# Down products of an eight-expert feed-forward layer with the weights stationary, turned back in the next block

## What is computed

```
h = jax.nn.silu(xf @ gw.T) * (xf @ uw.T)
eo = h @ dw.T
out = out + mask[:, None].astype(xf.dtype) * eo * mean_w
```

## Time and profile before

| | before |
|---|---|
| median of 3 runs | 470.59 us |
| the profiled execution's own time | 470.76 us |
| its span in the trace | 468.9 us |
| PE busy | 445.0 us, 95% of the span |
| DVE busy | 301.5 us |
| ACT busy | 278.3 us |
| GpSimd busy | 140.9 us |
| mean granted PE clock | 0.989 |

### The profile page before, as it was taken

The page is one execution under the profiler, slowest core; times in us unless marked ns, Lnnn a source line. Parts: engine busy times, 40 slices in busy tenths (PEclk is TensorE's granted clock), DMA queues, the critical chain, the costliest instruction groups (busy, mean ns, idle before and its releaser), DMA issues.

```text
span 468.9 us, 9096 instructions
## 1 busy us (share of the span) xinstructions
PE 445.0 (95%) x2825; PEld 366.2 (78%) x2825; DVE 301.5 (64%) x743; ACT 278.3 (59%) x886; POOL 140.9 (30%) x172
## 2 busy tenths in 40 slices
PE   7899999999999999899999999999999999999980
PEld 4566565666666665589999999999999999999980
DVE  3776879898988977877647466376464663763320
ACT  2488878878787788355456455454554554554230
POOL 5301116262727243663050130410501304105022
PEclk9999999999999999999999999999999999999995
DMA  5740182040303042436845565557455654113002
GB/s 160 227 108 5 49 313 73 5 112 8 109 11 107 11 123 65 121 105 181 277 85 155 166 129 143 141 151 213 78 148 167 130 148 95 17 40 41 1 8 31
DMA packets 24668, 49.92 MB, mean 106 GB/s; under 512 B 5730, under 2 KB 15494, under 8 KB 24474
## 3 DMA queue, kind: packets, MB, share of 16 engines
q1 hardware_dynamic: 12858, 22.95, 16.3%
q10 hardware_dynamic: 5616, 19.40, 13.9%
q0 software_dynamic: 6144, 6.97, 9.4%
HBM read 39.16 MB, written 13.20 MB: 112 GB/s over the span
## 4 chain that ended last, share of the span: by engine, by line
PE 73%; DVE 7%; DMA 6%; ACT 5%; issue 3%; POOL 2%; SPq 1%; ACTq 0%; POOLq 0%; DVEq 0%
PE b_small L779 9%; PE b_o L779 9%; PE b_s L764 7%; PE b_s L765 7%; PE b_s L768 7%; PE b_s L487 6%; PE b_pv L510 4%; ACT probs L912 3%; PE b_proj L566 3%; PE b_pt L496 3%; PE b_s L485 3%; PE b_pt L765 2%; PE b_pt L764 2%; PE b_pt L768 2%; PE b_proj L540 2%
## 5 line engine op out<-in xcount | busy, mean ns | idle before, releaser
L912 ACT ACTIVATE probs<-b_s,negmax 100x100 f32<-100x100 f32 x256 | 85.7, 361 | 19.3 <-DVE negmax L1230 19.1
L1452 POOL DMA_INDIRECT out<-y_sb,idnow x32 | 47.8, 1494 | 163.6 <-ACT y_sb L958 158.8
L945 ACT CAST h_hi<-h_sb 128x448 fp32r<-128x448 f32 x64 | 36.3, 567 | 87.1 <-DVE h_sb L1314 87.1
L764 PE MATMUL b_s<-x_hi,w_lo 128*128 128x448 f32 x192 | 70.6, 368 | 0.0
L765 PE MATMUL b_s<-x_hi,w_hi 128*128 128x448 f32 x192 | 69.7, 363 | 0.0
L768 PE MATMUL b_s<-x_lo,w_hi 128*128 128x448 f32 x192 | 69.2, 360 | 0.0
L1207 DVE TENSOR_TENSOR w_lo<-w_raw,w_hi 128x1024 fp32r<-128x1024 f32 x48 | 58.8, 1224 | 13.7 <-ACT w_hi L876 13.7
L1318 DVE TENSOR_TENSOR h_lo<-h_sb,h_hi 128x448 fp32r<-128x448 f32 x64 | 40.1, 626 | 40.5 <-ACT h_hi L945 40.5
L912 ACT ACTIVATION_READ_ACCUMULATOR probs<-b_s,negmax 100x1 f32 x256 | 56.9, 222 | 0.0
L487 PE MATMUL b_s<-kblk,qrot 128*100 128x400 f32 x128 | 53.6, 499 | 0.0
L876 ACT CAST w_hi<-w_raw 128x1024 fp32r<-128x1024 f32 x48 | 50.4, 1049 | 0.0
(11 more groups left out here) (180 smaller groups left out, 978.2 us busy)
## 6 DMA issues: line engine op xcount, KB each, us to landing
w_raw<-in_ffw ACTq DMA_DIRECT2D x36, 512.0 KB, 3.9
w_raw<-in_ffw SPq DMA_DIRECT2D x12, 512.0 KB, 5.5
slots<-in_padrows SPq DMA_DIRECT2D x9, 449.8 KB, 4.7
xin<-slots SPq DMA_DIRECT2D x9, 449.8 KB, 4.4
kblk<-krot SPq DMA_DIRECT2D x120, 12.5 KB, 1.8
out<-x_all SPq DMA_DIRECT2D x8, 200.0 KB
ctx_all<-in_ctxT SPq DMA_DIRECT2D x1, 1200.0 KB, 6.8
x_all<-in_x SPq DMA_DIRECT2D x1, 1200.0 KB
```

The source lines that it names most:

```text
L764: pe.matmul(o, wl[:, c, cols], x_hi[:, c, :], start=(c == 0), stop=False)
L912: m = nc.scalar.activation(probs[:, N % 3, h, :], b_s[N % 3][0:S, h * S:(h + 1) * S], ACT.Exp, bias=negmax[:, N % 4, h:h + 1], accum_out=p ...
L945: nc.scalar.copy(h_hi[:, f, :], h_sb[:, f % 2, :]).then_inc(s_hhi, 1)
L1452: G.indirect_dma_start(out, bass.IndirectOffsetOnAxis(idnow[:, n:n + 1], 0), y_sb[:, n, :], None, bounds_check=TOK + TILE - 1, oob_is_err= ...
```

## The change

The down product changes sides. The down weights are now stationary (128x128) and the 448 rows of `h` move, so that one chunk takes 6 matmuls (2 output column blocks c, 3 part products) and the result has output columns on the partitions: column block 0 in `b_o`, block 1 in `b_small`. ACT scales it into the new buffer `yT` (`take_columns`, 2 copies of 128x448). In the next block, behind `hidden` of f = 0, PE turns it back with 8 transposes (`output_transpose`) into `b_xt`, and ACT copies it behind its f = 0 work into `y_sb` (`take_rows`, 2 copies of 112x512). The last expert keeps the old `project_down` and `take_output`; its block still runs `output_transpose` and `take_rows` for the tile before it. The first block transposes a `yT` that nobody reads.

```diff
+            def columns_down(par, t, f, chunks=range(DC)):
+                pe.wait_ge(s_hlo, FC * t + f + 1)
+                if f == 0:
+                    pe.wait_ge(s_y, GRP * t + GRP)
+                wh, wl = wpart(w_hi[par])[2], wpart(w_lo[par])[2]
+                for c in chunks:
+                    for k, (left, right) in enumerate(((wh, h_hi), (wl, h_hi), (wh, h_lo))):
+                        m = pe.matmul(b_y[c][:, 0:TILE], left[:, f, c * P:(c + 1) * P], right[:, f, :],
+                                      start=(f == 0 and k == 0), stop=(f == FC - 1 and k == 2))
+                    if f == FC - 1:
+                        m.then_inc(s_down, 1)
+
+            def output_transpose(t):
+                pe.wait_ge(s_yT, DC * t + DC)
+                for g in range(GRP):
+                    for c in range(DC):
+                        m = pe.transpose(b_xt[g // 2][0:ROWS, g % 2 * D + c * P:g % 2 * D + (c + 1) * P],
+                                         yT[:, c, g * ROWS:(g + 1) * ROWS], ident[:, :])
+                    if g % 2:
+                        m.then_inc(s_yt, 1)
+
...
                     hidden(par, t, f)
+                    if f == 0:
+                        output_transpose(lo if last else t)
                     if f >= 3:
-                        project_down(par, t, f - 3)
+                        (project_down if last else columns_down)(par, t, f - 3)
+                if not last:
+                    for c in range(DC):
+                        for f in range(FC - 3, FC):
+                            columns_down(par, t, f, (c,))
+                    return
...
+            def take_columns(t, e):
+                a.wait_ge(s_mean, 1)
+                for c in range(DC):
+                    a.wait_ge(s_down, DC * t + c + 1)
+                    nc.scalar.activation(yT[:, c, :], b_y[c][:, 0:TILE], ACT.Copy, scale=meanw[:, e:e + 1]
+                                         ).then_inc(s_yT, 1)
+
+            def take_rows(t):
+                a.wait_ge(s_idnow, t)
+                for n in range(GRP // 2):
+                    a.wait_ge(s_yt, 2 * t + n + 1)
+                    nc.scalar.copy(y_sb[:, 2 * n:2 * n + 2, :].rearrange("p g d -> p (g d)"), b_xt[n][0:ROWS, :]
+                                   ).then_inc(s_y, 2)
...
                 for f in range(FC):
                     silu(t, f)
                     hidden_high(t, f)
+                    if f == 0 and follow:
+                        take_rows(t)
                     if split and f < WCH:
                         weights_high(e, par, f)
...
                 if e < E - 1:
-                    take_output(t, e)
+                    take_columns(t, e)
...
+            V.memset(yT[:, :, :].rearrange("p c t -> p (c t)"), 0.0).then_inc(s_yT, DC)
```

More of the change, by code:

```diff
@@ L223, in build @@
         y_sb = sb("y_sb", [ROWS, GRP, D])
+        yT = sb("yT", [P, DC, TILE])
         b_small = bank("b_small")
@@ L343, in build @@
         s_y = sem("s_y")
+        s_yT = sem("s_yT")
+        s_yt = sem("s_yt")
         s_add = sem("s_add")
@@ L783, in project_down, with block @@
                         m.then_inc(s_down, 1)
-            def block(t, par, last):
+            def columns_down(par, t, f, chunks=range(DC)):
[17 more added lines that the diff above has]
+                        m.then_inc(s_yt, 1)
+            def block(t, par, last, lo):
                 for f in range(FC):
@@ L800, in block @@
                 project_down(par, t, FC - 1, range(2, GRP))
-                if last:
-                    tile_transpose(t + 1)
+                tile_transpose(t + 1)
             warm(2)
@@ L809, in _ @@
                 with pe.Fori(lo, hi) as t:
-                    block(t, e % 2, e == E - 1)
+                    block(t, e % 2, e == E - 1, lo)
         @block.scalar
@@ L959, in take_output, with step @@
                                          ACT.Copy, scale=meanw[0:ROWS, e:e + 1]).then_inc(s_y, 1)
-            def step(t, e, par, split, again):
+            def take_columns(t, e):
[10 more added lines that the diff above has]
+                                   ).then_inc(s_y, 2)
+            def step(t, e, par, split, again, follow):
                 for f in range(FC):
@@ L974, in step @@
                 if e < E - 1:
-                    take_output(t, e)
+                    take_columns(t, e)
             def expert(e, par, again):
                 lo, hi, end = tiles_of(a, e)
-                step(lo, e, par, True, again)
+                step(lo, e, par, True, again, e > 0)
                 with a.If(end - lo), a.Fori(lo + 1, hi) as t:
-                    step(t, e, par, False, False)
+                    step(t, e, par, False, False, True)
             def last_expert(e, par):
-                lo, hi, _ = tiles_of(a, e)
-                with a.Fori(lo, hi) as t:
-                    step(t, e, par, False, False)
+                lo, hi, end = tiles_of(a, e)
+                step(lo, e, par, False, False, True)
+                with a.If(end - lo), a.Fori(lo + 1, hi) as t:
+                    step(t, e, par, False, False, False)
             x_high(0)
```

## The result

The changed kernel takes 467.24 us (median of 6 runs, 466.06 to 468.65), the kernel before 470.77 (6 runs, 470.26 to 472.55). The ratio is 0.9917 with a 95% interval of 0.9902 to 0.9931, so it is about 3.9 us faster (3.3 to 4.6); the two medians differ by 3.5. The forecast was 4.1 us less, 466.5, range 465.2 to 469.0.

A forecast was written before the change was run, and what follows sets the result against it. PE's instruction count and spacing were taken to bound the feed-forward blocks. Down products -11.48 us and new transposes +7.36 us gave -4.1 us, so 466.5 us was forecast, range 465.2 to 469.0.

The forecast's parts named there:

- Down products: On PE in seven blocks, 48 at 0.2002 us replace 96 short ones: 1.64 us less per block, 11.48 in all.
- Rival 2: Down products on PE miss the hidden matmuls' spacing, gaining about 1.40 us per block: 468.2 us; chance 0.02.
- New transposes: 8 more on PE in each of 8 blocks, 0.92 us per block, 7.36 in all; bounds 6.3 and 8.2.
- Rival 3: Transposes on PE not pipelined, 176 ns each, 11.3 us in all: no change, 470.4 us; chance 0.06.
- A full block: Blocks of experts 2 to 7: about 30.56 us, PE busy in all of it, against 31.28 before.
- The zero at f = 3: ACT 0.97 us late delays gated of f = 1; hidden of f = 3 keeps 0.58 us, no cost.
- The slack at f = 7: ACT's 0.73 us of waiting for PE is used up, but gated also waits for the up product: no cost.
- the tail: Block end: PE asks for h_lo of f = 7 after 2.40 us instead of 2.81, leaving 0.3 us of cover.
- Rival 1: PE waits for late ACT at f = 3 and the block's end, copies taking 0.9 us: 467.5 to 469.6; chance 0.09.
- The adds: A tile's adds start about 5 us into the next block, idnow copy ends at 15 to 18; about 6 us left.
- Rival 4: Late adds hold DVE at take_ids, so PE waits at block end: 473.5 us; or clock falls: 474; chance 0.05 together.
- the mark of 24.8: Microseconds into the block; an idnow copy ending later starts to cost, and outweighs the gain at 25.5.

The follow-up runs named there:

- double_copies: The changed kernel with each of the two take_rows copies preceded by another copy into free memory: 475.94 us, ratio 1.0021.
- no_turn: The changed kernel without the 8 output transposes, ACT still making its two copies: 462.97 us, ratio 0.9825.
- late_copies: The changed kernel with take_rows behind f = 3 instead of f = 0, without the down products' wait for y_sb: 472.90 us, ratio 1.0043.
- steady_start: The changed kernel with 14 idle matmuls instead of 8 on PE at the start: 471.78 us, ratio 0.9916.
- all_three: The changed kernel with the edits of no_first, early_load and steady_start together: 470.95 us, ratio 0.9909.
- no_first: The changed kernel without the first block's output transposes and without the clearing of yT: 466.88 us, ratio 0.9907.
- early_load: no_first with SP reading the next expert's two bounds before it waits for the scatters: 472.68 us, ratio 0.9947.
- turn_only: The kernel before with 8 unread transposes of a constant added behind hidden of f = 0 in all eight blocks: 477.97 us, ratio 1.0138.
- turn_ahead: The changed kernel with the output transposes ahead of hidden of f = 0 instead of behind it: 481.93 us, ratio 1.0132.
- after_again: The changed kernel once more, unedited, on the second chip: 472.85 us, ratio 0.9937.
- after_third: The changed kernel a third time, unedited, on the third chip: 472.29 us, ratio 0.9935.

## Why the prediction was right

- **Down products.** 0.200 us apart as forecast, so 48 of them in place of 96 short ones give 1.64 us a block. Rival 2 is out: a gain of 1.40 us would have made blocks of 30.76 us with the 0.88 measured for the transposes, and they are 30.475. That was also the estimate from the gap rule of the Trainium skill ("TensorE: Matmul & The Clock Gate", section Back-to-back issue gap).
- **New transposes.** 0.88 us (forecast 0.92, bounds 0.79 to 1.03), in both kernels that have them and in the one that has nothing else of the change. Their pace fits the moving columns, 0.108 us for 128 and 0.095 for 112; these are two forms only, which differ in their stationary side too, so the cause of the pace is not shown apart. Rival 3 (1.4 us) is out. The first row that speaks against it was there before: no load stood apart by its full length.
- **A full block.** 31.28 - 1.64 + 0.88 = 30.52, forecast 30.56, measured 30.475; the rest of 0.045 is half explained by the 0.02 us of the earlier trace rows that were in none of the three prices. The last block grew by 0.87, as its down products stay (forecast 0.92).
- **ACT.** 0.95 us late where 0.97 was forecast. The zero at f = 3 was right with less to spare than written: 0.58 forecast, 0.55 in the trace, 0.38 usable (`double_copies`). It is only there because the transposes delay PE too: `no_turn` waits 0.50 us (0.34 forecast; the 0.06 behind `gated` and the 0.10 of the second start are the difference). The slack at f = 7 was used up as said, and the tail has 0.32 left (0.3 forecast). Rival 1 is out, as the copies take 0.58 to 0.59 us, and `double_copies` shows how near it was.
- **The adds.** The `idnow` copy at 17.1 us, forecast 15 to 18; the 6 us of cover are 7.7 to the forecast's mark, and 8.4 to where `take_ids` really runs. Rival 4 did not happen, and `late_copies` shows that its chain exists. Its price was too high: 2.4 us beyond the mark of 24.8 cost 1.46 us in the block, not 2.4, since DVE only came to `take_ids` 25.5 us into it, 0.7 us behind the mark, and the covers of the tail took part of its wait of 1.78.
- **The clock.** 1.00 in all blocks, with 0.88 and 0.79 us of transposes in each. The rule of the Trainium skill ("TensorE: Matmul & The Clock Gate", section Part 4: PE-mode transpose), by which they don't count as busy, changed nothing at this length; whether it holds, such short stretches can't tell.
- **The sum.** In the eight blocks the two profiles differ by -1.06 - 4.83 + 0.87 = -5.0 us, against 7 x (0.92 - 1.64) + 0.92 = -4.1. Of the 0.9 between them, 8 x 0.04 = 0.3 are the transposes, 7 x 0.045 = 0.3 the rest of the full block, and 0.24 the wait for `xin` in the first block, which fell away. The later start gave back 1.47 us, more than these 0.9, and the profiled executions differ by 3.45 us, the medians by 3.5. So the forecast of 466.5 came within 0.7 us partly by luck: its blocks were 0.9 us too slow, and it had nothing for the part ahead of the first block. That part is not steady. With the clock at 1.00 from 10 to 20 and from 180 to 195 us the first block starts at 204.97 to 205.36 in five profiles (`no_turn`, `double_copies`, before, `late_copies`, `steady_start`). With a lower clock in one or both it starts at 205.61 to 207.03 in six (`all_three`, `no_first`, `early_load`, `turn_only`, after, `turn_ahead`). `after_again` (207.18) and `after_third` (207.15, with the clock at 1.00) are late by something else as well: ACT stands once in the attention stage, for 2.35 and 2.38 us, as it does in the first block. Since `double_copies`, `late_copies` and `steady_start`, which all have the change, start within 0.3 us of the kernel before, the change by itself doesn't make the start later; the executions of the result that were not profiled don't show theirs.

## What to carry to other kernels

Where PE is full, count its instructions by form and take the spacing of the same form from the same trace: three prices gave a block to 0.05 us. Work put on another engine ahead of a chain is free only up to the cover less about 0.16 us (measured in two kernels here), and that cover can come from work that the same change adds on PE, so price the parts both together and apart. When a saving falls into the first round of a loop, look for a load whose time is set by another engine's work ahead of the loop; once PE waits for that load, a saving ahead of it is worth nothing.

## What the hardware showed that was not expected

- A wait on PE cost about 0.10 us beyond the gap itself: the start behind it comes 0.30 to 0.31 us later in place of 0.20 (`no_turn`, `double_copies`, `late_copies`).
- Four indirect adds and their landing took 11.8 to 12.1 us beside the weight fetches and 9.6 in the seventh block, which has none.
- The granted clock from 10 to 20 us is 0.83 in two of the thirteen profiles, after and `turn_only`, and 1.00 in the others, so it does not come from the clearing of `yT`. What decides it is open.
- In all seven profiles of the second and third chip the first block was 34.8 to 37.7 us long, against 30.6 to 32.3 in the other six. ACT stood ahead of the silu of f = 1, for 5.07 and 5.06 us in `after_again` and `after_third` and for 0.7 to 4.4 in the others, in which it or DVE stood again behind that. The cause is open.
